# Graph layer and gated feed-forward: order of the left parts around the norm in the first phase

## The chip, the cores and the metric

One Trainium2 chip, one core. The metric is the device time of one execution in microseconds (us); the kernel before has 2005.67 us as the median of 3 runs (2003.96 to 2008.26).

## The reference

N = 10000 rows of D = 1024 numbers in float32, and 5000 edges (src, dst).

```
u   = layernorm(x)                            # per row
h   = u @ W.T + b                             # W 1024 x 1024
deg = 1 + count of src per row;  dis = deg ** -0.5
x1[i] = x[i] + sum over edges (i, j), with (i, i) added: dis[i] * dis[j] * h[j]
z   = layernorm(x1)
out = x1 + z @ base_W.T + base_b + z @ A_s.T @ B_s.T
      + sum over the best 2 of 6 experts: gate_e * (z @ A_e.T) @ B_e.T      # rank 16
```

## The kernel before

**Tiles and phases.** The rows are padded to 79 tiles of 128. The first phase makes, for every tile, the weighed rows h * dis (stored as `h_rows`, for the gathers) and the residual part (`r_rows`). The second phase gathers neighbours, normalises again and applies the feed-forward; it is not touched.

**Precision.** Every float32 matrix is split into a high part (a copy rounded to fp32r by ScalarE, `left_high`, `quarter_high`) and a low part (the difference, by VectorE, `left_low`, `quarter_low`). A product of high and low parts is three matmuls for each 128 rows of depth.

**The first phase.** The first HEAD = 7 tiles are done plainly: per tile, both halves of the output and all of depth, 48 matmuls (`single`). From tile 7 on, two tiles form a pair (36 pairs, `first(p) = 7 + 2p`), and a scheme of Strassen's kind needs 7 products of 512 x 512 blocks for 8. The left operands of a pair are A11, S1, S2, A12, S3, A22, S4, the right ones B11, T1, T2, B21, T3, T4, B22. The right sums T1 to T4 are made once, during the last plain tiles, by GpSimd (`quarter`), in four pieces of 128 x 512 each, then split by ScalarE and VectorE. A product is 12 matmuls (`product`, lines 1412 to 1416).

**The left operands.** For each tile: VectorE takes `statistics(t)`, GpSimd the power -1/2 of the variance (`rstd(t)`), VectorE makes `scales(t)`, ScalarE normalises the tile into `un` (`normalise(t)`, line 1048), and TensorE transposes it into the two banks `bt[0]` and `bt[1]` (line 1423), with `transpose_first(p)` for the first tile of a pair and `transpose_second(p)` for the other. From the first tile come A11 and A12. From the second, A21 is copied out of bt[0] (`second_row`), and A22 stays in bt[1] until both its parts are taken. `sums(p)` on VectorE makes S1, S2, S3, S4 and the low parts of S1 and S2; `sums_high(p)` on ScalarE the high parts of S1, S2 and A12; `others_high(p)` those of A22 and S3; `last_high(p)` that of S4. All are instructions at line 1089 (high) and 1892 (low).

**The order of TensorE** is fixed. Within pair p: S1, S2, first transposes of pair p+1, A12, S3, A11 of pair p+1, second transposes of pair p+1, A22, S4. The first transposes of p+1 wait for `un`, for A21 and for the low part of A22 of pair p, since they overwrite bt. S2 waits for a bank that ScalarE fills (`begin_second`).

**Queues.** Every engine runs its own list in order, with waits on semaphores. ScalarE's list for pair p, from the sums on: `begin_first(p+2)`, `begin_second(p+1)`, `second_row(p+1)`, `sums_high(p+1)`, `normalise(first(p+2))`, `weigh_part(p, C21, A22)`, `others_high(p+1)`, then `last_high(p+1)`. VectorE's, after `sums(p+1)`: statistics of first(p+2), low part of A12, scales of first(p+2), low parts of A22 and S3, then `finish_part`, S4, and the residual.

**Factors.** dis = deg ** -0.5 for 79 tiles is a power on GpSimd (`factors`, line 763), done in column groups FACTORS: tiles 0 to 7 at t = 2, the three others at t = 3, 4 and 5 of the plain tiles. VectorE makes sqd = deg * dis from it (line 1769). Pairs 1 to 20 also carry the ranking of edges (`ranks`) on VectorE, pairs 2 to 21 the counts on GpSimd, pair 22 the slot table, pair 24 the spill flag, which the transposes of the next pair wait for.

Of the kernel before, what the change touches and what calls it, by code (L numbers as in the profile page):

```python
# [10 lines left out]
ALU = mybir.AluOpType  # L11
# [7 lines left out]
TILES = -(-N // P)  # L19
# [34 lines left out]
HEAD = 7  # L54
# [26 lines left out]

T_AT = {T3: 4, T1: 8, T2: 12, T4: 16}

FACTORS = ((0, 8), (8, 32), (32, 56), (56, TILES))
RANK_AT, COUNT_AT, SLOT_AT, SCATTER_AT, TABLE_AT = 1, 2, 22, 23, 28


# [71 lines left out]
def gnn_ffn(nc, x, src, dst, w_t, b, base_t, b_low, router_b, out, deg_dram, spill_dram):  # L159
# [5 lines left out]
    with ExitStack() as ctx:  # L165
# [287 lines left out]
        def first(p):  # L453

            return HEAD + 2 * p
# [254 lines left out]
        def _(pool):  # L710
# [55 lines left out]
            for t in range(HEAD):  # L766
                if t == 2:
                    pool.wait_ge(deg_ok, 1)
                    factors(*FACTORS[0])
                rstd(t + 2)  # L770
                if t == 3:
                    pool.wait_ge(t_in[1], 16)
                    pool.wait_ge(t_in[0], 32)
                    quarter(wr_raw[T3], wr_raw[T3], wr_raw[T1], 0)
                if t == 4:
                    quarter(wr_raw[T1], wr_raw[T1], wr_high_raw[T1], 1)
                if 3 <= t < 3 + len(FACTORS) - 1:
                    factors(*FACTORS[t - 2])
                if t == 5:
                    pool.wait_ge(t_ok, 8)  # L780
                    pool.wait_ge(t_in[2], 32)
                    quarter(wr_raw[T2], wr_high_raw[T2], wr_raw[T1], 2)
                if t == 6:
                    pool.wait_ge(t_ok, 12)
                    quarter(t4, t4, wr_raw[T2], 3)
# [47 lines left out]
            for p in range(PAIRS):  # L833
                if p + 1 < PAIRS:
                    rstd(first(p + 1) + 1)
                if 0 <= p - COUNT_AT < CHUNKS // RANKED:
                    gather_counts(p - COUNT_AT)
                if SCATTER_AT <= p < SCATTER_AT + CHUNKS // 10:
                    c = 10 * (p - SCATTER_AT)
                    if p == SCATTER_AT:  # L840
                        pool.wait_ge(zero_stored, 64)
                        pool.wait_ge(slots_ok, 1)
                        carry_wait(12)
                    put_slots(range(c, c + 5))
                if p + 2 < PAIRS:
                    rstd(first(p + 2))
                if 0 <= p - COUNT_AT < CHUNKS // RANKED:
                    put_counts(p - COUNT_AT)
                if SCATTER_AT <= p < SCATTER_AT + CHUNKS // 10:
                    put_slots(range(c + 5, c + 10))  # L850
                if 0 <= p - PIECE_AT < PIECES:
                    differences(p - PIECE_AT)
# [186 lines left out]
        def _(act):  # L1039
# [134 lines left out]
            def weigh_sum(p, n, t, to, v, ok):  # L1174

                act.wait_ge(done, product_at(p, n))
                if p > 0:
                    act.wait_ge(part_ok[v], p)
                else:
                    act.wait_ge(t_lo_ok, 16)  # L1180
                nc.scalar.activation(to[:], bp[p % 2][1][:], ACT.Copy,
                                     scale=dis[:, first(p) + t:first(p) + t + 1]).then_inc(ok, 1)

            def weigh_part(p, v, n):

                t, h = PARTS[v]
                act.wait_ge(done, product_at(p, n))
                if p == 0:
                    act.wait_ge(dis_ok, len(FACTORS))
                    act.wait_ge(r_ok, HEAD - 1 + (t == 0))  # L1190
                    act.wait_ge(h_stored[t], 16 * ((HEAD - 1 - t) // 2 + 1))
                else:
                    act.wait_ge(part_stored[v], 16 * p)
                    act.wait_ge(pair_r_ok, 2 * (p - 1) + t + 1)
                nc.scalar.activation(hrow[t][:, half(h)], bp[p % 2][BANK[n]][:], ACT.Copy,
                                     scale=dis[:, first(p) + t:first(p) + t + 1]) \
                    .then_inc(part_ok[v], 1)
# [44 lines left out]
                    quarter_high(T2, wr_raw[T2])  # L1242
            second_row(0)
            sums_high(0)
            normalise(first(1))
            weigh(HEAD - 1)
            begin_second(0)
            others_high(0)
            begin_first(1)
            act.wait_ge(first_done, 2 * HEAD)  # L1250
            act.wait_ge(t_ok, 16)
            quarter_high(T4, t4)

            for p in range(PAIRS):
                last_high(p)
                if p == PAIRS - 1:
                    right_high(B11)
                weigh_sum(p, S2, 0, u2, C12, u2_ok)
                if p + 1 < PAIRS:
                    first_row(p + 1)  # L1260
                weigh_part(p, C11, A12)
                if p + 1 < PAIRS:
                    first_row_right(p + 1)
                    normalise(first(p + 1) + 1)
                    if p > 0:
                        begin_third(p + 1)
                weigh_sum(p, S3, 1, u3, C22, u3_ok)
                if p + 2 < PAIRS:
                    begin_first(p + 2)
                if p + 1 < PAIRS:  # L1270
                    begin_second(p + 1)
                    second_row(p + 1)
                    sums_high(p + 1)
                if p + 2 < PAIRS:
                    normalise(first(p + 2))
                weigh_part(p, C21, A22)
                if p + 1 < PAIRS:
                    others_high(p + 1)

            act.wait_ge(weights_in[7], 48)  # L1280
            nc.scalar.activation(narrow_hi[:], narrow_raw[:], ACT.Copy).then_inc(rest_hi_ok, 1)
# [423 lines left out]
        def _(dve):  # L1705
# [43 lines left out]
            def quarter_low(n, raw, at):  # L1749
                for k in range(4):  # L1750
                    dve.wait_ge(t_hi_ok, at + k + 1)
                    if n in (T1, T2):
# [2 lines left out]
                                            wr_hi[n][:, k, :].bitcast(F32), ALU.subtract) \  # L1755
                        .then_inc(t_lo_ok, 1)

            def finish_rows(t):

                if t == 0:  # L1760
                    dve.wait_ge(rows_in, 32)
                    dve.wait_ge(dis_ok, 1)
                    link(nc.vector.tensor_tensor(sqd[:, 0:HEAD], deg[:, 0:HEAD], dis[:, 0:HEAD],
                                                 ALU.mult))
                    nc.vector.tensor_tensor(b_step[:], b_rows[:, half(1)], b_rows[:, half(0)],
                                            ALU.subtract).then_inc(step_ok, 1)
                if t == HEAD - 1:
                    dve.wait_ge(dis_ok, len(FACTORS))
                    link(nc.vector.tensor_tensor(sqd[:, HEAD:TILES], deg[:, HEAD:TILES],
                                                 dis[:, HEAD:TILES], ALU.mult))  # L1770
                dve.wait_ge(h0_ok, 2 * (t + 1))
                nc.vector.scalar_tensor_tensor(hrow[t % 2][:], b_rows[:], dis[:, t:t + 1],
                                               hrow[t % 2][:], ALU.mult, ALU.add).then_inc(h_ok, 1)
                dve.wait_ge(h_ok, t + 1)
                nc.vector.scalar_tensor_tensor(xn[t % 6][:], xn[t % 6][:], sqd[:, t:t + 1],
                                               hrow[t % 2][:], ALU.mult, ALU.add).then_inc(r_ok, 1)
# [164 lines left out]
            for t in range(HEAD):  # L1941
# [21 lines left out]
                    columns()  # L1963
                if t == 4:
                    quarter_low(T3, wr_raw[T3], 0)
                if t == 5:
                    quarter_low(T1, wr_raw[T1], 4)
                if t == HEAD - 1:
                    left_low(0, A11, a11[:])
                    quarter_low(T2, wr_raw[T2], 8)  # L1970
            sums(0)
            statistics(first(1))
            left_low(0, A12, left_raw[A12][:])
            scales(first(1))
            left_low(0, A22, bt[1][:])
            dve.wait_ge(s3_ok, 1)
            left_low(0, S3, left_raw[S3][:])

            for p in range(PAIRS):
                if p == 0:  # L1980
                    finish_rows(HEAD - 1)
                    quarter_low(T4, t4, 12)
                else:
                    finish_part(p - 1, C12, S4, u2, u2_ok)
                left_low(p, S4, s4[:])
# [9 lines left out]
                    scales(first(p + 1) + 1)  # L1995
                if p > 0:
                    residual(p - 1, 1, (C22, C21))
                if RANK_AT <= p < RANK_AT + CHUNKS // RANKED:
                    ranks(p - RANK_AT)
                if p == SLOT_AT:  # L2000
# [4 lines left out]
                if p + 1 < PAIRS:  # L2005
                    sums(p + 1)
                    if p + 2 < PAIRS:
                        statistics(first(p + 2))
                    left_low(p + 1, A12, left_raw[A12][:])
                    if p + 2 < PAIRS:  # L2010
                        scales(first(p + 2))
                    left_low(p + 1, A22, bt[1][:])
                    dve.wait_ge(s3_ok, p + 2)
                    left_low(p + 1, S3, left_raw[S3][:])
            finish_part(PAIRS - 1, C12, S4, u2, u2_ok)
# [323 lines left out]
```

## Time and profile before

| | before |
|---|---|
| median of 3 runs | 2005.67 us |
| profiled execution, its own time | 2003.67 us |
| its span | 2001.5 us |
| TensorE busy | 1926.3 us, 96% |
| VectorE, ScalarE, GpSimd busy | 73%, 45%, 48% |
| granted TensorE clock, mean | 0.987 |
| plain tiles | to about 109 us |
| pairs | to about 880 us |
| second phase | the rest |

The granted clock is the share of full speed that TensorE got. A busy time counts an instruction from its start to its modelled end; matmuls overlap, so 390 ns of one is not its price: in sequence they start 0.23 us apart at full clock.

### The profile page before, as it was taken

How to read it: one execution, taken by the hardware profiler on the slowest of the kernel's cores; microseconds unless marked ns; L12 is line 12 of the kernel's file. 1: busy time of each engine (PE TensorE's matmuls, PEld its weight loads, DVE VectorE, ACT ScalarE, POOL GpSimd, SP SyncE). 2: the span in 40 equal slices, each digit the busy share in tenths (PEclk: the TensorE clock that was granted, in tenths of full speed). 3: DMA queues.
4: the chain of work that ended last, by engine and by line, in shares of the span. 5: the costliest groups of instructions: out<-in, count | busy, mean ns of one | idle time of the engine just before them, and what ended most of it. 6: DMA issues, size and time to landing. Idle time of an engine off the chain costs nothing.

```text
span 2001.5 us, 28823 instructions
## 1 busy us (share of the span) xinstructions
PE 1926.3 (96%) x9583; PEld 1613.6 (81%) x9583; DVE 1463.7 (73%) x3528; ACT 906.8 (45%) x1533; POOL 952.5 (48%) x963
## 2 busy tenths in 40 slices
PE   7989999999999999966999999999999999999999
PEld 6778777877787888855788888888888888888887
DVE  6878788878877667758677777767767766776775
ACT  4455555555555556543433433434343343434332
POOL 1712444354333520027655665656566665556640
PEclk9989999999999999987999999999999999999999
DMA  6624555545534444475333433333333333343321
GB/s 241 212 92 170 164 174 179 182 160 172 192 139 145 166 136 163 147 256 145 88 99 101 106 88 97 93 106 101 104 98 92 95 93 105 97 108 95 91 63 54
DMA packets 148969, 260.54 MB, mean 130 GB/s; under 512 B 56077, under 2 KB 75357, under 8 KB 148822
## 3 DMA queue, kind: packets, MB, share of 16 engines
q1 hardware_dynamic: 99478, 237.85, 34.1%
q0 software_dynamic: 49344, 20.85, 8.3%
q8 instruction: 77, 1.26, 0.3%
q14 instruction: 70, 0.57, 0.1%
HBM read 273.80 MB, written 129.74 MB: 202 GB/s over the span
## 4 chain that ended last, share of the span: by engine, by line
PE 63%; issue 19%; POOL 11%; DVE 4%; DMA 2%; ACT 1%; POOLq 0%; SPq 0%; DVEq 0%; ACTq 0%
PE bo L1552 13%; PE bo L1556 13%; PE bo L1554 13%; PE bt L1602 3%; POOL piece L829 3%; POOL counted L796 2%; PE bo L1412 2%; PE bo L1416 2%; PE bo L1414 2%; POOL xpw L738 2%; POOL counts L810 2%; PE bo L1570 2%; PE bo L1566 2%; PE bo L1568 2%; PE bo L1592 2%
## 5 line engine op out<-in xcount | busy, mean ns | idle before, releaser
L860 POOL DMA_INDIRECT acc<-h_rows,row_now x308 | 503.8, 1636 | 104.4 <-issue 101.7
L1412 PE MATMUL bo<-wr_hi,left_hi 128*128 128x512 f32 x1008 | 399.6, 396 | 4.8 <-ACT bo L1164 3.1
L1416 PE MATMUL bo<-wr_hi,left_lo 128*128 128x512 f32 x1008 | 393.7, 391 | 0.0
L1414 PE MATMUL bo<-wr_lo,left_hi 128*128 128x512 f32 x1008 | 393.0, 390 | 0.0
L738 POOL TENSOR_TENSOR xpw<-xpin,neg_half 128x1 f32<-128x1 f32 x79 | 72.7, 920 | 489.4 <-DVE xpin L1720 489.4
L1552 PE MATMUL bo<-wr_hi,sum_hi 128*128 128x512 f32 x624 | 248.2, 398 | 2.3 <-DVE sum_lo L2164 2.3
L1554 PE MATMUL bo<-wr_lo,sum_hi 128*128 128x512 f32 x624 | 244.6, 392 | 0.0
L1556 PE MATMUL bo<-wr_hi,sum_lo 128*128 128x512 f32 x624 | 244.4, 392 | 0.0
L1412 PEld LDWEIGHTS bo<-wr_hi,left_hi 128*128 128x128 f32 x1008 | 189.7, 188 | 42.9 <-issue 5.9
L1416 PEld LDWEIGHTS bo<-wr_hi,left_lo 128*128 128x128 f32 x1008 | 189.6, 188 | 40.2
L1414 PEld LDWEIGHTS bo<-wr_lo,left_hi 128*128 128x128 f32 x1008 | 189.8, 188 | 37.2
L948 POOL TENSOR_TENSOR pw<-pin,neg_half 128x1 f32<-128x1 f32 x79 | 73.6, 932 | 273.9 <-DVE pin L2081 262.2
L1048 ACT ACTIVATE un<-xn,xshift,xscale 128x1024 f32<-128x1024 f32 x79 | 98.3, 1244 | 229.3 <-issue 228.5
L1294 ACT ACTIVATE z_half<-acc,shift,scale 128x512 f32<-128x512 f32 x158 | 119.8, 807 | 91.5 <-DVE shift L2099 91.5
L1556 PEld LDWEIGHTS bo<-wr_hi,sum_lo 128*128 128x128 f32 x624 | 117.8, 189 | 25.6
L1552 PEld LDWEIGHTS bo<-wr_hi,sum_hi 128*128 128x128 f32 x624 | 117.7, 189 | 25.5 <-ACT row_hi L1301 3.0
L1554 PEld LDWEIGHTS bo<-wr_lo,sum_hi 128*128 128x128 f32 x624 | 117.9, 189 | 22.0
L1552 PE MATMUL bo<-wr_hi,right_hi 128*128 128x512 f32 x320 | 132.1, 413 | 0.2 <-DVE acc L2182 0.2
L1556 PE MATMUL bo<-wr_hi,right_lo 128*128 128x512 f32 x320 | 125.1, 391 | 0.0
L1554 PE MATMUL bo<-wr_lo,right_hi 128*128 128x512 f32 x320 | 124.7, 390 | 0.0
L2188 DVE TENSOR_TENSOR sum_raw<-bt,row_raw 128x512 f32<-128x512 f32 x39 | 27.0, 691 | 133.0 <-ACT row_raw L1337 133.0
L2173 DVE SCALAR_TENSOR_TENSOR acc<-acc,dis,bo 128x512 f32<-128x512 f32 x158 | 117.1, 741 | 4.3 <-PE bo L1596 3.1
(235 smaller groups left out, 4281.9 us busy)
## 6 DMA issues: line engine op xcount, KB each, us to landing
xn<-x SPq DMA_DIRECT2D x79, 512.0 KB, 3.9
r_rows<-xn SPq DMA_DIRECT2D x79, 512.0 KB, 3.3
acc<-r_rows SPq DMA_DIRECT2D x79, 512.0 KB, 4.4
out<-acc SPq DMA_DIRECT2D x79, 512.0 KB, 2.8
h_rows<-hrow SPq DMA_DIRECT2D x144, 256.0 KB, 2.3
acc<-h_rows,row_now POOLq DMA_INDIRECT x308, 4.3
wr_raw<-w_t SPq DMA_DIRECT2D x16, 256.0 KB, 6.4
piece<-base_t SPq DMA_DIRECT2D x64, 64.0 KB, 2.8
```

The lines of the kernel that those rows point to most:

```text
L738: nc.gpsimd.tensor_tensor(xpw[t % 2][:], xpin[t % 2][:], neg_half[:, 0:1], ALU.pow) \
L860: nc.gpsimd.indirect_dma_start(to[:], None, h_dram, bass.IndirectOffsetOnAxis(ap=at, axis=0), bounds_check=NPAD - 1, oob_is_err=False, com ...
L948: nc.gpsimd.tensor_tensor(pw[:], pin[:], neg_half[:, 0:1], ALU.pow) \
L1048: nc.scalar.activation(un[:], xn[t % 6][:], ACT.Identity, bias=xshift[t % 2][:], scale=xscale[t % 2][:]) \
L1294: ins = nc.scalar.activation(z_half[v][:], acc[a][:, half(v)], ACT.Identity, bias=shift[:], scale=scale[:])
L1412: nc.tensor.matmul(ps, left_hi[n][:, k, :], wr_hi[n][:, k, :], start=False, stop=False, skip_group_check=True)
L1414: nc.tensor.matmul(ps, left_hi[n][:, k, :], wr_lo[n][:, k, :], start=False, stop=False, skip_group_check=True)
L1416: last = nc.tensor.matmul(ps, left_lo[n][:, k, :], wr_hi[n][:, k, :], start=False, stop=(k == 3), skip_group_check=True)
L1552: nc.tensor.matmul(ps, y_hi[n][:, k, :], wr_hi[w][:, k, :], start=(begins and k == 0), stop=False, skip_group_check=True)
L1554: nc.tensor.matmul(ps, y_hi[n][:, k, :], wr_lo[w][:, k, :], start=False, stop=False, skip_group_check=True)
L1556: last = nc.tensor.matmul(ps, y_lo[n][:, k, :], wr_hi[w][:, k, :], start=False, stop=(k == 3), skip_group_check=True)
L2173: nc.vector.scalar_tensor_tensor(av, av, dis[:, bass.ds(t, 1)], bank, ALU.mult, ALU.add).then_inc(f_ok, 1)
```

## The change

- ScalarE, loop: `others_high(p+1)` stands directly behind `sums_high(p+1)`, ahead of `normalise(first(p+2))` and `weigh_part(p, C21, A22)`.
- VectorE, loop: the low part of A22 stands ahead of `scales(first(p+2))`.
- ScalarE, start: `begin_second(0)`, `others_high(0)` and T4's high parts stand ahead of the norm of tile 9 (`first(1)`), of `weigh(6)` and `begin_first(1)`.
- VectorE, start: T1's low parts move from t = 5 to t = 6; A12, A22 come ahead of the statistics of tile 9, S3 ahead of its scales; T4's low parts ahead of the rows of tile 6.
- GpSimd: the groups are tiles 0 to 7, 8 to 15, 16 to 47 and 48 to 78. The second is done at t = 3, the third and fourth in pairs 0 and 1, between the powers for two norms.
- sqd follows in two pieces; ScalarE waits on the factors' semaphore where it first needs each group.

```diff
-FACTORS = ((0, 8), (8, 32), (32, 56), (56, TILES))
+FACTORS = ((0, 8), (8, 16), (16, 48), (48, TILES))
+
+LATER_AT, LATER = (0, 1), (16 - HEAD) // 2
...
-                if 3 <= t < 3 + len(FACTORS) - 1:
-                    factors(*FACTORS[t - 2])
+                if t == 3:
+                    factors(*FACTORS[1])
...
+                if p in LATER_AT:
+                    factors(*FACTORS[2 + LATER_AT.index(p)])
                 if p + 2 < PAIRS:
                     rstd(first(p + 2))
...
                 else:
                     act.wait_ge(t_lo_ok, 16)
+                    act.wait_ge(dis_ok, 2)
+                if p == LATER:
+                    act.wait_ge(dis_ok, len(FACTORS))
...
                 if p == 0:
-                    act.wait_ge(dis_ok, len(FACTORS))
                     act.wait_ge(r_ok, HEAD - 1 + (t == 0))
...
             second_row(0)
             sums_high(0)
-            normalise(first(1))
-            weigh(HEAD - 1)
             begin_second(0)
             others_high(0)
-            begin_first(1)
             act.wait_ge(first_done, 2 * HEAD)
             act.wait_ge(t_ok, 16)
             quarter_high(T4, t4)
+            normalise(first(1))
+            weigh(HEAD - 1)
+            begin_first(1)
...
                     sums_high(p + 1)
+                    others_high(p + 1)
                 if p + 2 < PAIRS:
                     normalise(first(p + 2))
                 weigh_part(p, C21, A22)
-                if p + 1 < PAIRS:
-                    others_high(p + 1)
...
+            def later_factors(a, z, n):
+                dve.wait_ge(dis_ok, n)
+                link(nc.vector.tensor_tensor(sqd[:, a:z], deg[:, a:z], dis[:, a:z], ALU.mult))
...
                 if t == HEAD - 1:
-                    dve.wait_ge(dis_ok, len(FACTORS))
-                    link(nc.vector.tensor_tensor(sqd[:, HEAD:TILES], deg[:, HEAD:TILES],
-                                                 dis[:, HEAD:TILES], ALU.mult))
+                    later_factors(HEAD, FACTORS[2][0], 2)
...
-                if t == 5:
+                if t == HEAD - 1:
                     quarter_low(T1, wr_raw[T1], 4)
-                if t == HEAD - 1:
                     left_low(0, A11, a11[:])
                     quarter_low(T2, wr_raw[T2], 8)
             sums(0)
+            left_low(0, A12, left_raw[A12][:])
+            left_low(0, A22, bt[1][:])
             statistics(first(1))
-            left_low(0, A12, left_raw[A12][:])
-            scales(first(1))
-            left_low(0, A22, bt[1][:])
             dve.wait_ge(s3_ok, 1)
             left_low(0, S3, left_raw[S3][:])
+            scales(first(1))
+            quarter_low(T4, t4, 12)
...
                     finish_rows(HEAD - 1)
-                    quarter_low(T4, t4, 12)
...
+                if p == LATER - 1:
+                    later_factors(FACTORS[2][0], TILES, len(FACTORS))
...
                     left_low(p + 1, A12, left_raw[A12][:])
+                    left_low(p + 1, A22, bt[1][:])
                     if p + 2 < PAIRS:
                         scales(first(p + 2))
-                    left_low(p + 1, A22, bt[1][:])
```

## Rows read from the trace of the kernel before

**Rows 1.** Page, part 1: busy us, share of the span, instructions.

```profile
PE 1926.3 (96%) x9583; PEld 1613.6 (81%) x9583; DVE 1463.7 (73%) x3528; ACT 906.8 (45%) x1533; POOL 952.5 (48%) x963
```

**Rows 2.** Table by stretch: length, busy of each engine, PEclk, DMA share, GB/s.

```profile
101.40:108.20 6.80, 5.90 (x18) 5.03 (x19) 4.97 (x7) 4.11 (x8) 4.17 (x3) 0.50 0.32 107
...
118.50:121.90 3.40, 3.40 (x10) 2.51 (x9) 3.33 (x6) 2.95 (x6) 0.00 (x0) 0.50 0.14 58
...
142.70:599.60 456.90, 441.67 (x2101) 364.38 (x2101) 369.86 (x890) 251.68 (x400) 184.91 (x246) 1.00 0.50 170
```

**Rows 3.** Timeline of TensorE, start of the pairs: start, duration, instruction, idle before.

```profile
102.30 1.97 PE L1423 MATMUL bt<-ident,un 128*128 128x128 f32 x8 [3.19 <-ACT un L1048]
...
108.78 0.39 PE L1412 MATMUL bo<-wr_hi,left_hi 128*128 128x512 f32 x1
...
117.45 0.47 PE L1412 MATMUL bo<-wr_hi,left_hi 128*128 128x512 f32 x1 [3.07 <-ACT bo L1164]
```

**Rows 4.** Waits of TensorE, 142.7 to 853.3 us: total, times, longest.

```profile
PE bt L1423 <- DVE left_lo L1892: 16.2, 22, 1.1
PE bt L1423 <- DVE spill_flag L1989: 1.8, 1, 1.8
```

**Rows 5.** Timeline of TensorE: transposes, pairs 1, 2, 23, 34 and 35.

```profile
121.83 1.07 PE L1423 MATMUL bt<-ident,un 128*128 128x128 f32 x8
...
130.94 1.03 PE L1423 MATMUL bt<-ident,un 128*128 128x128 f32 x8
...
142.71 1.03 PE L1423 MATMUL bt<-ident,un 128*128 128x128 f32 x8
...
599.60 1.03 PE L1423 MATMUL bt<-ident,un 128*128 128x128 f32 x8
...
832.41 1.04 PE L1423 MATMUL bt<-ident,un 128*128 128x128 f32 x8
...
853.27 1.03 PE L1423 MATMUL bt<-ident,un 128*128 128x128 f32 x8
```

**Rows 6.** Timeline of ScalarE in a pair without stall.

```profile
589.93 1.88 ACT L1089 ACTIVATE left_hi<-left_raw 128x512 fp32r<-128x512 f32 x3 [0.82 <-DVE left_raw L1907]
596.37 1.25 ACT L1048 ACTIVATE un<-xn,xshift,xscale 128x1024 f32<-128x1024 f32 x1 [4.56 <-issue]
...
598.09 0.58 ACT L1089 ACTIVATE left_hi<-bt 128x512 fp32r<-128x512 f32 x1
```

**Rows 7.** Timeline of VectorE: A22's low part, pairs 5 and 6.

```profile
228.04 0.69 DVE L1892 TENSOR_TENSOR left_lo<-bt,left_hi 128x512 fp32r<-128x512 f32 x1 [2.42 <-ACT left_hi L1089]
...
250.15 0.69 DVE L1892 TENSOR_TENSOR left_lo<-bt,left_hi 128x512 fp32r<-128x512 f32 x1 [2.42 <-ACT left_hi L1089]
```

**Rows 8.** Timeline of GpSimd: powers for factors, and one for a norm.

```profile
46.51 1.65 POOL L763 TENSOR_TENSOR dis<-deg,neg_half 128x8 f32<-128x8 f32 x1 [18.36 <-DVE deg L1950]
...
77.88 4.62 POOL L763 TENSOR_TENSOR dis<-deg,neg_half 128x24 f32<-128x24 f32 x1
...
83.64 4.82 POOL L763 TENSOR_TENSOR dis<-deg,neg_half 128x23 f32<-128x23 f32 x1
...
138.06 0.93 POOL L738 TENSOR_TENSOR xpw<-xpin,neg_half 128x1 f32<-128x1 f32 x1 [10.34 <-DVE xpin L1720]
```

**Rows 9.** Timeline of VectorE in the last plain tiles and pair 0.

```profile
60.66 2.00 DVE L1772 SCALAR_TENSOR_TENSOR hrow<-b_rows,dis,hrow 128x1024 f32<-128x1024 f32 x1 [0.98 <-ACT hrow L1070]
...
86.25 0.16 DVE L1729 SCALAR_TENSOR_TENSOR xshift<-xmv,xscale 128x1 f32<-128x1 f32 x1
89.82 5.69 DVE L1754 TENSOR_TENSOR wr_lo<-wr_raw,wr_hi 128x512 fp32r<-128x512 f32 x4 [3.41 <-ACT wr_hi L1082]
...
107.25 0.68 DVE L1907 TENSOR_TENSOR left_raw<-bt,a 128x512 f32<-128x512 f32 x1
```

**Rows 10.** Timeline of ScalarE around tile 9's norm.

```profile
97.14 0.58 ACT L1109 ACTIVATE left_raw<-bt 128x512 f32<-128x512 f32 x1
...
114.43 1.24 ACT L1048 ACTIVATE un<-xn,xshift,xscale 128x1024 f32<-128x1024 f32 x1 [4.59 <-issue]
```

## The prediction

> **What bounds the kernel now.** I read the page's busy shares first: TensorE is busy 96% of the span [rows 1], so time can only come from its idle stretches and from stretches at a low clock. The table by stretch says where these lie inside the first phase. From 142.7 to 599.6 us the engine is busy 441.67 of 456.90 us at clock 1.00, so 15.2 us are idle; two short stretches near the start, 6.80 and 3.40 us, run at granted clock 0.50 [rows 2]. That is the lower of the engine's two levels, 1.2 GHz against 2.4, and each stretch comes with a stall, of 3.19 and of 3.07 us [rows 3]. The table of waits names what is late in the pair loop: 22 times the transposes wait for the low part of a left matrix, 16.2 us in all, and once for the spill flag, 1.8 us [rows 4]. All three are at the lines that the change moves.
>
> Below, "first transposes of pair p+1" are those that fill both banks bt again; they must wait until VectorE has read the A22 block of pair p out of bt[1], which it does in the low part of A22. "Second transposes" are the other tile's.
>
> **The loop's price now.** The first transposes of pairs 34 and 35 start at 832.41 and 853.27 [rows 5], 20.86 us apart with no wait, which I take as the period of an unhindered pair. From pair 2 (142.71) to pair 35 (853.27) there are 33 periods in 710.56 us; at 20.86 they would be 688.4. So 22.2 us are lost. (The waits of [rows 4] add up to 18.0; the rest is the array filling again, some 0.2 us after each.)
>
> **Why the low part is late.** A pair without the ranking work shows the queue on ScalarE: three high parts end at 591.81, it idles 4.56 us, does the norm at 596.37, weighs a part, and only at 598.09 takes A22's high part [rows 6]. The norm waited for its scales, which VectorE and GpSimd make from the statistics. VectorE in turn idles 2.42 us before A22's low part, in pairs with ranking too (228.04 and 250.15) [rows 7]. A22's high part needs nothing of the norm: its source is in bt[1] since the second transposes, and its buffer is free after one product that follows them. So it waits only because of its place in the queue.
>
> **Part 1, pair loop (others_high ahead of normalise; A22's low part ahead of scales).** In the pair of [rows 6], A22's high part would run at about 591.8 instead of 598.09, and its low part right behind A12's, near 595.4 instead of 598.7, where it follows the high part: 3.3 us earlier. The largest single wait is 1.1 us [rows 4], so all 22 go, with 2 us to spare. What is late next? First VectorE itself. In a ranking pair its cycle is 250.15 - 228.04 = 22.11 us, of which 2.42 is that idle time and about 0.5 the wait for the scales that A22's low part now fills: 19.2 us of work and short waits, under 20.86, so TensorE sets the period. Second the norm. It moves behind two more copies on ScalarE, 0.58 us and about 0.6, but these run in the 4.56 us in which ScalarE idled, so they cost nothing; if that cover were gone they would cost 1.2. The scales move behind one low part of 0.6 us, 0.5 of it inside the wait for GpSimd's power; net 0.15 to 0.6. The norm of [rows 6] ends at 597.6 and the transposes that need it start at 599.60 [rows 5]: 2.0 us of cover against 0.15 to 1.8. Third the spill flag (pair 24): VectorE's queue ahead of it gets about 1.1 us shorter, no more, since S4's high part still follows the norm; about 0.7 us of loss stays. A period's part between first and second transposes is 9.11 us early on (121.83 to 130.94) and some 0.04 less in the last pairs; over 22 pairs that is 0.9, which stays. Gain of the loop: 22.2 - 0.7 - 0.9 = 20.6 us. Bounds: 0 if VectorE's work and not its wait is what binds, 22.2 above; below nothing only by the norm, see the rivals.
>
> **Part 2, the start.** Four edits meet here, so I follow the queues.
> - GpSimd loses 16 columns of power at t=3, and all of those at t=4 and t=5. Eight columns take 1.65 us, 24 take 4.62 [rows 8], 0.19 a column, so about 3.0 + 4.6 + 4.8 us of its queue go. The quarter sums T2 and T4 start some 5 and 8 us sooner.
> - VectorE has the four low parts of T1 (5.69 us, at 89.82 [rows 9]) no longer ahead of the statistics of tile 8. What takes their place is the two row operations of tile 5, now near 93.7, which run 2.0 to 2.2 us each where GpSimd subtracts quarters beside them, as the one at 60.66 [rows 9]. Scales then near 98.0; ScalarE has its copy of A12 done at 97.7 (97.14 + 0.58) [rows 10]; norm to 99.3. TensorE reaches these second transposes at 102.30 - 3.19 = 99.1 and starts them at 99.4, 2.9 us sooner, without the drop to half clock. A11 of pair 0, now at 108.78 [rows 3], follows 0.8 us of transposes and 12 matmuls of 0.23 later: 103.0.
> - VectorE makes up T1's low parts (2.5), A11's (0.7) and T2's (2.5) from 98.0 to 103.7, so the sums start at 103.7, not 107.25 [rows 9], and S1 is ready 3.25 us on, behind four sums of 0.6 each and its low part of 0.7: 106.95. TensorE, through with A11 at 105.7, waits 1.2 for it: a new, smaller stall. S1 ends 109.7.
> - S2 waited 3.07 us for the second bank [rows 3], because ScalarE sat 4.59 us before the norm of tile 9 at 114.43 [rows 10]. begin_second now comes first; this stall and its half-clock stretch go. S2 ends at 112.4.
> - Then the norm of tile 9 is late. From 106.3 VectorE has five low parts (S1, S2, A12, A22, S3) and the statistics (1.9) ahead of its scales, to 111.3; GpSimd's power 111.7, scales 112.05, norm 113.35. First transposes of pair 1 at 113.45, against 121.83 [rows 5]: 8.4 us sooner, with a stall of 1.0.
> - VectorE goes on without a pause: low parts of T4 2.5, square roots 0.3, rows of tile 6 2.6, S4 0.6, statistics 1.9, A11 of pair 1 0.7: 120.7. TensorE wants it at 119.8, a last stall of 0.95. Second transposes of pair 1 at 123.5, against 130.94 [rows 5]: gain 7.4 us.
> - The powers of 32 and 31 columns, 5.5 to 6.1 us by the rates above, run on GpSimd in pairs 0 and 1 between two powers for norms; its idle time there is 10.34 us before 138.06 [rows 8]. Hidden; without cover they would cost up to 6 us each. Square roots of later tiles, done in pair 3: 0.2 us of VectorE, hidden by its idle time. The added waits on dis_ok are met long before, and nothing queues behind them. No DMA is added, and SyncE's order is as it was; row stores of tile 6 come no later than its queue needs.
>
> Bounds of this part: 2.9 (only S2's stall goes and tile 8's norm stays late) to 10.
>
> **Sum.** 7.4 + 20.6 = 28.0 us. The second phase starts from the last stores of the first and is shifted whole. The profiled execution took 2003.67 us, so 1975.7; the median of the runs is 2.0 above it, so the median forecast is 2005.67 - 28.0 = 1977.7.
>
> **A rule that speaks against it.** Beside the power of 23 columns (83.64 to 88.46), the scalar-tensor operation at 86.25, which reads two tiles of SBUF, took 0.16 us [rows 9]: not held at all; beside GpSimd's subtractions VectorE's low parts took 5.69 for four. The Trainium skill ("SBUF — State Buffer", "SBUF: two separate sides") says the port pair shared by VectorE and GpSimd is an exclusive lock for a whole instruction. By that the long powers would hold VectorE in pairs 0 and 1. The slowed low parts fit the rule; the power does not.
>
> **Rivals.**
> 1. The wait moves to the norm or to VectorE's work and half of the loop's gain stays: 1977.7 + 10.3 = 1988.0. For it: 65 norms wait for scales, and the ranking pairs leave VectorE only 1.7 us. Against: 2.42 us of idle time directly ahead of the late operation. 0.12.
> 2. At the start tile 8's norm stays late, since GpSimd's quarters now run beside VectorE's row operations: gain 2.9 instead of 7.4, 1982.2. 0.11.
> 3. The powers hold VectorE for 6 us in pairs 0 and 1, 2 of it covered each time: 8 us, 1985.7. The rule of the page named above would give this; the row at 86.25 speaks against. 0.03.
> 4. Slower: the norm slips in every pair. If it ends over 2.0 us later than now, each further us costs 34, once a pair. It needs ScalarE's 1.2 and VectorE's 0.6 in series and another 0.2 or more; at 3.0 us late the loop loses 34 in place of its present 22.2, and the start's 7.4 stay: 2005.7 - 7.4 - 22.2 + 34 = 2010. Against: 4.56 us of idle time. 0.05.
> 5. No effect: VectorE's order is not what binds, and the start only trades stalls. 2005.7. 0.03.
> The forecast itself has 0.66, with its own range 1973 to 1982.
>
> **Chances.** Faster by over 0.2% (4 us; less can't be told from no change here): 0.66 + 0.12 + 0.11 + 0.03 = 0.92. Within: 0.03. Slower: 0.05. The range reaches from 1973 (both upper bounds nearly) past rivals 2 and 3 to most of 1: 1989.
>
> **What would show it.** Right: no wait of the transposes for a low part between 120 and 850 us; a period of 20.86 to 20.9 in ranking pairs; the second transposes of pair 1 near 123.5; no stretch at clock 0.50 before 850 us; A22's high part directly behind A12's, with ScalarE's idle time before the norm shorter by 1.2. Wrong: waits for "un" at the first transposes of many pairs (rivals 1, 4), a stall of over 1 us near 99 (rival 2), or VectorE operations of several us beside the powers (rival 3).

## The result, and the profile after

| | before | changed |
|---|---|---|
| median | 2004.82 us (4 runs) | 1974.19 us (4 runs, 1973.28 to 1975.08) |
| ratio, 95% interval | | 0.984 (0.9829 to 0.9852) |
| span of the profiled run | 2001.5 us | 1972.0 us |

The forecast was 1977.7 us, within 1973 to 1989, faster. The time lies in the range, 1.2 us above its low end: 30.6 us were gained by the medians where 28.0 were forecast. Between the two profiled runs the span fell by 29.5 us.

The table by stretch, cut at the same events in both kernels: the first transposes of pair 0, the second of pair 1, the second of pair 35, and the end. Columns: stretch, length, busy time of TensorE, its weight loads, VectorE, ScalarE and GpSimd, granted clock, DMA share, GB/s. Before:

```profile
95.30:130.90 35.60, 29.34 (x121) 23.68 (x120) 26.74 (x48) 20.03 (x33) 10.08 (x7) 0.86 0.28 100
130.90:862.30 731.40, 713.45 (x3402) 590.45 (x3401) 564.13 (x1283) 407.64 (x645) 253.99 (x317) 1.00 0.48 160
862.30:2001.50 1139.20, 1100.93 (x5653) 931.66 (x5651) 801.60 (x2074) 439.38 (x793) 644.77 (x596) 0.98 0.38 103
```

After:

```profile
95.40:122.20 26.80, 25.35 (x122) 20.23 (x121) 23.35 (x45) 19.81 (x33) 5.10 (x4) 1.00 0.34 118
122.20:832.70 710.50, 709.55 (x3402) 592.37 (x3401) 562.67 (x1285) 405.39 (x646) 256.28 (x319) 1.00 0.50 166
832.70:1972.00 1139.30, 1099.99 (x5653) 931.52 (x5651) 801.27 (x2073) 439.50 (x793) 645.01 (x596) 0.98 0.37 103
```

The start is 8.8 us shorter, the loop 20.9, and what follows is as long as it was: the second phase is shifted whole. TensorE idles 0.95 us in 710.5 us of loop, and the start has clock 1.00 throughout, so both half-clock stretches of [rows 2] are gone. From pair 2 to pair 23 the first transposes now start 20.86 us apart, in every pair, ranking or not; that is the period of an unhindered pair in the prediction. I call the first length "the start" and the second "the loop" from here on.

The waits of TensorE after, from 90 to 850 us (total, times, longest), answer [rows 4]:

```profile
PE bt L1428 <- DVE spill_flag L1995: 1.0, 1, 1.0
PE bo L1417 <- issue: 0.9, 2, 0.6
PE bt L1428 <- ACT un L1052: 0.5, 1, 0.5
```

No transpose waits for a low part. The 0.9 and 0.5 us lie in the start. ScalarE in a ranking pair after (start, duration, instruction, idle before); it answers [rows 6]:

```profile
228.55 1.88 ACT L1093 ACTIVATE left_hi<-left_raw 128x512 fp32r<-128x512 f32 x3 [0.82 <-DVE left_raw L1914]
230.34 0.58 ACT L1093 ACTIVATE left_hi<-bt 128x512 fp32r<-128x512 f32 x1
230.81 0.62 ACT L1093 ACTIVATE left_hi<-left_raw 128x512 fp32r<-128x512 f32 x1
235.05 1.25 ACT L1052 ACTIVATE un<-xn,xshift,xscale 128x1024 f32<-128x1024 f32 x1 [3.62 <-issue]
```

A22's high part (from bt) runs directly behind the three others. The idle time before the norm has shrunk from 4.56 to 3.62 us (0.94, where 1.2 was the forecast sign): two copies went into time that was free. VectorE beside it, answering [rows 7]:

```profile
234.00 0.68 DVE L1899 TENSOR_TENSOR left_lo<-bt,left_hi 128x512 fp32r<-128x512 f32 x1
234.60 0.14 DVE L1733 COPY xscale<-xpw 128x1 f32<-128x1 f32 x1
```

Both the 2.42 us of idle time ahead of the low part [rows 7] and the 0.47 us ahead of the scales are gone. The latter stood in the trace before as:

```profile
225.28 0.15 DVE L1728 COPY xscale<-xpw 128x1 f32<-128x1 f32 x1 [0.47 <-POOL xpw L738]
```

At the start, TensorE after, answering [rows 3] and [rows 5]: second transposes of pair 0, A11, S1, first and second transposes of pair 1.

```profile
99.07 1.04 PE L1428 MATMUL bt<-ident,un 128*128 128x128 f32 x8
...
102.69 0.39 PE L1417 MATMUL bo<-wr_hi,left_hi 128*128 128x512 f32 x1
...
106.19 0.47 PE L1417 MATMUL bo<-wr_hi,left_hi 128*128 128x512 f32 x1 [0.61 <-issue]
...
112.44 1.09 PE L1428 MATMUL bt<-ident,un 128*128 128x128 f32 x8 [0.53 <-ACT un L1052]
...
122.18 1.04 PE L1428 MATMUL bt<-ident,un 128*128 128x128 f32 x8
```

The prediction had 99.4, 103.0, 106.95, 113.45 and 123.5 for these five.

### The profile page after: what moved, and what is told of

Its sections match the earlier page's. It is cut to its first block, busy times and chain, and to the rows that moved or that the text cites. A ratio compares the mean times of both kernels' runs of the same rounds, so it can differ in the third digit from the quotient of the medians.

```text
span 1972.0 us, 28823 instructions
## 1 busy us (share of the span) xinstructions
PE 1917.8 (97%) x9583; PEld 1612.4 (82%) x9583; DVE 1458.1 (74%) x3529; ACT 904.6 (46%) x1533; POOL 945.1 (48%) x963
## 3 DMA queue, kind: packets, MB, share of 16 engines
q8 instruction: 77, 1.26, 0.3%
## 4 chain that ended last, share of the span: by engine, by line
PE 91%; issue 2%; POOL 2%; DVE 1%; ACT 1%; DMA 0%; POOLq 0%; DVEq 0%; ACTq 0%
PE bo L1557 13%; PE bo L1561 13%; PE bo L1559 13%; PE bo L1417 11%; PE bo L1421 11%; PE bo L1419 11%; PE bt L1607 4%; PE bt L1428 3%; PE bo L1575 2%; PE bo L1571 2%; PE bo L1573 2%; PE bo L1597 2%; PE bo L1599 2%; PE bo L1601 2%; POOL wr_raw L760 1%
## 5 line engine op out<-in xcount | busy, mean ns | idle before, releaser
L1559 PEld LDWEIGHTS bo<-wr_lo,sum_hi 128*128 128x128 f32 x624 | 117.6, 189 | 21.9
```

Source lines behind the costliest of these rows:

```text
L1559: nc.tensor.matmul(ps, y_hi[n][:, k, :], wr_lo[w][:, k, :], start=False, stop=False, skip_group_check=True)
```

## The experiments

Beside each time stand the lengths of the start and the loop, read in its trace as above (before 35.6 and 731.4, changed 26.8 and 710.5). They tell apart what the times blur, but each comes from one profiled execution. Ratios are to the kernel before on the same chip, with their 95% interval.

**The two parts apart.** loop_only is the kernel before with this edit alone:

```diff
                     sums_high(p + 1)
+                    others_high(p + 1)
...
-                if p + 1 < PAIRS:
-                    others_high(p + 1)
...
+                    left_low(p + 1, A22, bt[1][:])
                     if p + 2 < PAIRS:
                         scales(first(p + 2))
-                    left_low(p + 1, A22, bt[1][:])
```

> The kernel before with the two moves inside the pair loop alone (A22's and S3's high parts ahead of the norm on ScalarE, A22's low part ahead of the scales on VectorE). Theory: the gain of the loop and that of the start simply add, because a late low part of A22 costs TensorE once per pair whatever the start was. The second transposes of pair 1 stay at 130.9 us, both stretches at half clock stay, no wait of the transposes for a low part is left; gain 20.9 us, 1983.9 against 2004.8. Rival: the ranking pairs only run without stall because the start left VectorE further ahead; then part of the waits stays and the gain is under 15 us, over 1990.

Measured: 1982.38 us, 0.9887 (0.9871 to 0.9904); start 36.9, loop 709.9. The loop gives up 21.5 us whatever the start was.

start_only is the changed kernel with that edit undone:

> The changed kernel with the two moves inside the pair loop undone; start and factors as changed. Theory: second transposes of pair 1 at 122.2 us, no stretch at half clock before 850 us, but the 22 waits for a low part (16 us) and the spill flag's 1.8 us are back; gain 8.8 us, 1996.0. Rival: the earlier start gives VectorE and ScalarE a lead that takes some waits away, gain over 12 us.

Measured: 1996.62 us, 0.9958 (0.9942 to 0.9975); start 26.8, loop 731.5. The waits before the transposes are back: 22 of them, 18.2 us in all, where there were 23 with 18.0 us before (the spill flag's included). The trace names the low part for 9 of them and nothing for the other 13. The two gains, 22.1 and 7.9 us by the medians, add to 30.0 of the 30.6: they are independent. The rival (a lead carries over) falls.

In loop_only the start is 1.3 us longer than before. The same two stalls (3.18 and 3.77 us there) came with half-clock stretches of 3.4 and 6.8 us instead of 6.8 and 3.4. All of the 1.3 us lies behind the second stall, where the longer stretch falls: from S2 to the second transposes of pair 1 it is 14.8 us (118.66 to 133.42), and 13.5 before (117.45 to 130.94):

```profile
104.50:107.90 3.40, 3.40 (x11) 2.68 (x10) 3.39 (x4) 2.02 (x4) 2.28 (x2) 0.53 0.51 154
107.90:118.20 10.30, 6.77 (x29) 4.93 (x27) 6.99 (x16) 4.35 (x7) 0.93 (x1) 0.99 0.01 2
118.20:125.00 6.80, 6.34 (x18) 5.11 (x19) 5.87 (x9) 4.45 (x9) 0.00 (x0) 0.52 0.35 140
```

**Which engine's order pays in the loop.** late_scales takes back VectorE's half of the edit:

```diff
                     left_low(p + 1, A12, left_raw[A12][:])
-                    left_low(p + 1, A22, bt[1][:])
                     if p + 2 < PAIRS:
                         scales(first(p + 2))
+                    left_low(p + 1, A22, bt[1][:])
```

> The changed kernel with VectorE's order in the loop as before: A22's low part behind the scales of the next norm; ScalarE's order stays changed. Theory: ScalarE's order is the whole of the loop's gain. A22's low part comes 0.7 to 0.9 us later in each pair but still over 2 us ahead of the transposes; VectorE idles 0.45 us more for GpSimd's power, its cycle in ranking pairs near 19.7 us, under TensorE's 20.86. Time as changed, 1974.2 within 1. Rival: VectorE's order carries a part of it; then waits of up to 0.5 us come back in the ranking pairs, 1979 to 1984.

Measured: 1973.52 us, 0.9843 (0.9826 to 0.9859); start 26.8, loop 709.7, no wait of TensorE in the loop. With ScalarE's order changed, VectorE's half of the edit adds nothing that can be measured. (VectorE's half alone can't run: its low part of A22 would wait for ScalarE's high part, which stands behind the norm, which waits for the scales, which would stand behind that low part.)

**How much cover the norm has.** The fourth rival said that it slips. norm_late5 and norm_late10 put 5 and 10 useless copies of S3's high part ahead of the real one, and so ahead of the norm, in 34 pairs:

```diff
                 free_after(p, S3)
+                if p > 1:
+                    act.wait_ge(s3_ok, p + 1)
+                    for i in range(5):
+                        nc.scalar.activation(left_hi[S3][:].rearrange("p k n -> p (k n)"),
+                                             left_raw[S3][:], ACT.Copy).then_inc(ends_ok, 1)
+                        act.wait_ge(ends_ok, 5 * (p - 2) + i + 2)
                 left_high(p, S3, left_raw[S3][:], s3_ok, p + 1)
```

(norm_late10 has 10 in place of both 5s.)

> The changed kernel with five further copies of S3's high part on ScalarE ahead of the real one, in 34 pairs; they delay the norm. Theory: the norm waits for its scales, not for ScalarE, and has 3.6 us of idle time before it; five copies with their waits take about 3.5 us. The norm moves by 0 to 0.3 us, which the 2 us before the transposes cover: 1974.2 within 1. Rival: ScalarE's queue ahead of the norm is on the path; then each pair costs up to 3.5 us, 2090.

> The changed kernel with ten further copies of S3's high part ahead of the real one in 34 pairs. Five took 3.5 us and cost nothing. Theory (a cover of 2 us behind ScalarE's 3.6 us of idle time): ten take 7 us, the norm ends 3.4 us later than in the changed kernel, 1.4 us after TensorE is ready for the first transposes; with the array's filling again 1.6 us a pair, 54 us in all: 2028, within 15. Rival: the cover is larger, since everything else would shift with it: under 10 us lost. Other rival: the second norm and S4 slip too and each pair costs the full 3.4 us, 2090.

Measured: 5 copies 1974.35 us, 0.9842 (0.9825 to 0.9858), loop 709.5; 10 copies 2029.92 us, 1.0117 (1.0101 to 1.0132), loop 762.8. ScalarE with 5 copies:

```profile
230.48 3.28 ACT L1146 ACTIVATE left_hi<-left_raw 128x512 fp32r<-128x512 f32 x5
233.79 0.63 ACT L1093 ACTIVATE left_hi<-left_raw 128x512 fp32r<-128x512 f32 x1
234.72 1.25 ACT L1052 ACTIVATE un<-xn,xshift,xscale 128x1024 f32<-128x1024 f32 x1 [0.29 <-DVE xshift L1740]
```

with 10 copies, and TensorE's waits with 10:

```profile
238.94 6.60 ACT L1146 ACTIVATE left_hi<-left_raw 128x512 fp32r<-128x512 f32 x10
245.57 0.63 ACT L1093 ACTIVATE left_hi<-left_raw 128x512 fp32r<-128x512 f32 x1
246.11 1.22 ACT L1052 ACTIVATE un<-xn,xshift,xscale 128x1024 f32<-128x1024 f32 x1
```

```profile
PE bt L1434 <- ACT un L1052: 40.0, 30, 1.9
PE bt L1434 <- DVE spill_flag L2001: 3.2, 1, 3.2
```

Five use up the idle time (0.29 us left of 3.62) and cost nothing. Ten make the time 55.6 us longer than five do, against 54 forecast for ten; 53.3 us of it lie in the loop, 1.6 a pair, and the rest behind the loop, where no experiment looked. In the changed kernel the norm ends 1.95 us before the transposes that need it, in nearly every pair; with ten copies it ends 0.05 us before them. So the cover is the idle time plus this 1.95 us, and the mechanism of rival 4 (the norm slips) is real, but lay far off.

**The powers beside VectorE.** power_beside adds, in pairs 4 to 19, a power of 28 columns whose result is not used:

```diff
+                if 4 <= p < 20:
+                    nc.gpsimd.tensor_tensor(tick_pool[:, 16:44], deg[:, 0:28],
+                                            neg_half[:, 0:28], ALU.pow)
                 if p + 2 < PAIRS:
                     rstd(first(p + 2))
```

> The changed kernel with a further power of 28 columns on GpSimd (result not used) in each of pairs 4 to 19, between the powers for two norms. Theory: a power on GpSimd does not hold VectorE; it takes about 4.8 us of GpSimd's idle time, VectorE's operations beside it keep their length, time as changed, 1974.2 within 1. Rival (exclusive lock of the shared port for a whole instruction): VectorE's operations with two operands in SBUF wait up to 4.8 us in each of 16 pairs, of which about 2 are covered: some 40 us more, 2015.

Measured: 1974.15 us, 0.9837 (0.9821 to 0.9854); start 26.8, loop 709.6. GpSimd's power, and VectorE's operations inside it:

```profile
203.85 5.13 POOL L850 TENSOR_TENSOR tick_pool<-deg,neg_half 128x28 f32<-128x28 f32 x1
```

```profile
205.69 0.75 DVE L1879 SCALAR_TENSOR_TENSOR hrow<-bo,dis,u 128x512 f32<-128x512 f32 x1
207.21 0.69 DVE L1917 TENSOR_TENSOR left_raw<-bt,a 128x512 f32<-128x512 f32 x1 [0.77 <-ACT a L1123]
207.94 0.69 DVE L1922 TENSOR_TENSOR left_raw<-left_raw,a 128x512 f32<-128x512 f32 x1
```

The last has both operands in SBUF and took 0.69 us, its length without a power beside it. The Trainium skill ("SBUF — State Buffer", "SBUF: two separate sides") states that a VectorE operation with two SBUF inputs and a GpSimd operation that reads SBUF exclude each other for the whole instruction. This power reads SBUF and the rule does not hold for it; rival 3 is out. VectorE's low parts do get slower beside GpSimd's 512-column subtractions, below.

**What the start's 8.8 us are made of.** Three kernels take parts of the start back. t1_early moves T1's low parts back to t = 5:

```diff
-                if t == HEAD - 1:
+                if t == 5:
                     quarter_low(T1, wr_raw[T1], 4)
+                if t == HEAD - 1:
                     left_low(0, A11, a11[:])
```

> The changed kernel with T1's low parts back at t = 5 on VectorE, ahead of the statistics of tile 8. Theory: since GpSimd's quarters are now early, T1's high parts are ready near 88.9 and the low parts no longer wait 3.4 us; they end near 93.5, scales of tile 8 near 98.5, second transposes of pair 0 near 100.0 instead of 99.07, sums near 103.3 instead of 102.75: 0.5 to 1 us lost, 1975. Rival: the place of T1's low parts is what freed tile 8's norm; then the second transposes come at 102 again, with a half-clock stretch, and over 4 us are lost.

Measured: 1974.04 us, 0.9841 (0.9824 to 0.9857); start 27.7, loop 709.6. That is 0.9 us in the trace, under what the time can tell. The second transposes of pair 0 start at 98.80, without a stall, though T1's low parts are again ahead of tile 8's statistics: T1's place is worth little once the factors have moved.

early_factors puts the powers back into the plain tiles and keeps all orders (its groups there are 8, 32 and 31 columns, where the kernel before had 24, 24 and 23):

```diff
-                if t == 3:
-                    factors(*FACTORS[1])
+                if 3 <= t < 3 + len(FACTORS) - 1:
+                    factors(*FACTORS[t - 2])
...
-                if p in LATER_AT:
-                    factors(*FACTORS[2 + LATER_AT.index(p)])
```

> The changed kernel with the power of the later factors back in the plain tiles on GpSimd (8, 32 and 31 columns at t = 3, 4 and 5). Theory: the quarter sums T2 and T4 move back by 5 to 6 us; T2's does no harm, but T4's then runs until about 102 beside T1's low parts, which take about 5 us instead of 2.5: sums at 105 instead of 102.75, about 2.3 us lost, 1976.5. Rival: the place of the factors does not matter and T1's place does: less than 0.5 us lost.

Measured: 1977.48 us, 0.9856 (0.984 to 0.9872); start 31.7, loop 709.5: 4.9 us lost in the trace, twice the forecast (by the ratios 3 us). The second transposes of pair 0 have a stall again:

```profile
101.36 1.09 PE L1426 MATMUL bt<-ident,un 128*128 128x128 f32 x8 [1.25 <-ACT un L1050]
```

GpSimd in this kernel:

```profile
78.84 5.89 POOL L765 TENSOR_TENSOR dis<-deg,neg_half 128x32 f32<-128x32 f32 x1
...
85.96 5.27 POOL L765 TENSOR_TENSOR dis<-deg,neg_half 128x31 f32<-128x31 f32 x1
91.21 6.99 POOL L760 TENSOR_TENSOR wr_raw<-wr_high_raw,wr_raw 128x512 f32<-128x512 f32 x4
98.16 0.54 POOL L740 TENSOR_TENSOR xpw<-xpin,neg_half 128x1 f32<-128x1 f32 x1
98.67 6.43 POOL L760 TENSOR_TENSOR t<-t,wr_raw 128x512 f32<-128x512 f32 x4
```

and VectorE:

```profile
93.03 1.80 DVE L1777 SCALAR_TENSOR_TENSOR hrow<-b_rows,dis,hrow 128x1024 f32<-128x1024 f32 x1 [3.86 <-ACT hrow L1072]
94.86 2.19 DVE L1780 SCALAR_TENSOR_TENSOR xn<-xn,sqd,hrow 128x1024 f32<-128x1024 f32 x1
98.74 0.15 DVE L1731 COPY xscale<-xpw 128x1 f32<-128x1 f32 x1 [1.68 <-POOL xpw L740]
98.93 1.05 DVE L1732 SCALAR_TENSOR_TENSOR xshift<-xmv,xscale 128x1 f32<-128x1 f32 x1
99.90 5.76 DVE L1757 TENSOR_TENSOR wr_lo<-wr_raw,wr_hi 128x512 fp32r<-128x512 f32 x4
```

The norm's power stands behind T2's subtractions (VectorE waits 1.68 us for it), then T1's low parts run beside T4's subtractions and take 5.76 us instead of 2.5. This accounts for the loss: up to the start of T1's low parts VectorE has lost 1.7 us against the changed kernel (99.90 against 97.32, in a trace that runs 0.9 us later as a whole), and the stretched low parts add 3.3. In the changed kernel the powers are out of the way and T4's subtractions are over at 96.1, before T1's low parts begin:

```profile
90.04 6.02 POOL L760 TENSOR_TENSOR t<-t,wr_raw 128x512 f32<-128x512 f32 x4
...
119.61 5.43 POOL L765 TENSOR_TENSOR dis<-deg,neg_half 128x32 f32<-128x32 f32 x1
```

factors_only is the reverse: factors moved and the loop changed, both queues' start orders as before:

> The changed kernel with both queues' start orders as before (ScalarE: norm of tile 9 and weigh(6) ahead of begin_second and A22; VectorE: T1's low parts at t = 5, A22 and T4 late); the factors stay moved and the loop stays changed. With early_factors (orders changed, factors back, 4.9 us lost at the start) it splits the start's 8.8 us. Theory: S2's stall of about 3 us and its half-clock stretch are back, the norm of tile 8 is still earlier than before; from the first transposes of pair 0 to the second of pair 1 about 31 us (35.6 before, 26.8 changed): 4 us lost, 1978. Rival: the factors' place is nearly the whole of the start's gain and the orders add little: under 1.5 us lost.

Measured: 1980.25 us, 0.9873 (0.9858 to 0.9888); start 32.7, loop 709.5: 5.9 us lost, where 4 were expected. S2's stall is back, and the granted clock is 0.50 for 6.8 us from 112.0, near its end. But the second transposes of pair 0 start without a stall, and T1's low parts, which stand ahead of tile 8's statistics as before, take 2.97 us instead of 5.69 [rows 9]. TensorE (second transposes of pair 0, S2) and VectorE (T1's low parts):

```profile
98.86 1.05 PE L1428 MATMUL bt<-ident,un 128*128 128x128 f32 x8
...
113.69 0.77 PE L1417 MATMUL bo<-wr_hi,left_hi 128*128 128x512 f32 x1 [3.78 <-ACT bo L1168]
```

```profile
88.76 2.97 DVE L1759 TENSOR_TENSOR wr_lo<-wr_raw,wr_hi 128x512 fp32r<-128x512 f32 x4 [1.88 <-ACT wr_hi L1086]
```

The stall of 3.19 us ahead of these transposes [rows 3] thus goes with the factors alone, while the orders alone (early_factors) leave 1.25 us of it. Of the start's 8.8 us the factors alone bring 2.9 (35.6 to 32.7), the orders alone 3.9 (35.6 to 31.7), and together 2.0 more than their sum.

**Further gains.** flag_early puts the spill flag's two instructions ahead of `finish_part`:

```diff
             for p in range(PAIRS):
+                if p == SLOT_AT + 2:
+                    dve.wait_ge(max_done, 1)
+                    link(nc.vector.tensor_reduce(over_max[0:1, :], bt[0][0:1, 0:P], AX.X, ALU.max))
+                    nc.vector.tensor_copy(spill_flag[:], over_max[0:1, :]).then_inc(tables_ok, 1)
                 if p == 0:
...
                 left_low(p, S4, s4[:])
-                if p == SLOT_AT + 2:
-                    dve.wait_ge(max_done, 1)
-                    link(nc.vector.tensor_reduce(over_max[0:1, :], bt[0][0:1, 0:P], AX.X, ALU.max))
-                    nc.vector.tensor_copy(spill_flag[:], over_max[0:1, :]).then_inc(tables_ok, 1)
```

> The changed kernel with VectorE's two instructions for the spill flag (pair 24) ahead of finish_part and of S4's low part. Theory: TensorE's one wait left in the loop (0.95 us before the transposes at 615.0) goes and nothing takes its place: about 1.1 us less, 1973.1. Rival: the reduction waits for its source and holds VectorE, so the stall moves: no gain or a loss of up to 1 us.

Measured: 1973.91 us, 0.9849 (0.9833 to 0.9866); start 26.7, loop 709.4. No wait is left, but most of the other profiles with the flag in its old place show none either (late_scales: loop 709.7), so the time gained nothing measurable. Pair 24 takes 21.02 us here, 21.11 to 21.42 in those profiles and 22.12 in the changed kernel's, where VectorE's sums of that pair started late, for no reason that the trace names.

fill_idle fills the idle time that VectorE still had before the rows of tile 5:

```diff
                 if t != 2:
                     statistics(t + 2)
+                if t == HEAD - 1:
+                    statistics(first(1))
...
+                    second_row(0)
                     act.wait_ge(t_ok, 12)
                     quarter_high(T2, wr_raw[T2])
-            second_row(0)
...
                     left_low(0, A11, a11[:])
-                    quarter_low(T2, wr_raw[T2], 8)
             sums(0)
+            quarter_low(T2, wr_raw[T2], 8)
             left_low(0, A12, left_raw[A12][:])
             left_low(0, A22, bt[1][:])
-            statistics(first(1))
+            scales(first(1))
             dve.wait_ge(s3_ok, 1)
             left_low(0, S3, left_raw[S3][:])
-            scales(first(1))
```

> A try to improve on the changed kernel at the start: VectorE takes the statistics of tile 9 in its 3.9 us of idle time before the rows of tile 5 (at 88.8), ScalarE copies A21 ahead of T2's high parts, VectorE makes the sums ahead of T2's low parts. Theory: the stalls of 0.61 (S1) and 0.53 us (first transposes of pair 1) go, and VectorE, which bounds the start, is 1.9 us further: second transposes of pair 1 1.5 us earlier, 1972.7; seen in the trace, hardly in the time. Rival: T2's low parts become the wait of S2 and what is gained at S1 is lost there: no change.

Measured: 1972.61 us, 0.983 (0.9817 to 0.9844); start 24.8, loop 710.6 (the flag's wait was there, 0.96 us). The start has no stall left. The edit of both is these two together:

> fill_idle and flag_early together. Theory: they add, since they touch different pairs: start as in fill_idle (24.8 us from the first transposes of pair 0 to the second of pair 1, 26.8 changed), and no wait for the spill flag in any run, where two of the profiles so far showed 0.95 us and the others none. Some 2 to 3 us less than changed: ratio to before 0.983, 1971.5 to 1972.5. Rival: nothing of the 2 us survives to the end, since the second phase waits for something not shifted: ratio 0.9845.

Measured: 1970.21 us (1969.37 to 1971.02), 0.9825 (0.9812 to 0.9838); start 24.8, loop 709.4. TensorE's only wait from 90 to 850 us stands at 848.4, behind the loop:

```profile
PE bo L1417 <- ACT u L1188: 0.9, 1, 0.9
```

Start and loop together are 3.1 us shorter than the changed kernel's in the traces (734.2 against 737.3); 1.1 of it is pair 24, long in that one profile. Both kernels beat the one before clearly. The two were not timed side by side: their times do not overlap (1969.37 to 1971.02 against 1973.28 to 1975.08), but the intervals of their ratios do, so that the combined version is faster than the changed kernel is likely, and shown by the traces better than by the times.

## Where the prediction held, and which step of it failed

- **What bounds the loop**: right. TensorE waited for A22's low part because of its place in ScalarE's queue. The loop lost 22.2 us by the working; it gave back 20.9 in the profiled run and 21.5 to 22.0 in nine other profiles with ScalarE's new order in the loop (709.4 to 709.9, two of them with the flag moved).
- **The step that failed** is in the start, in two parts. The first is the cause of tile 8's late norm. The prediction has it freed because T1's low parts no longer stand ahead of its statistics, and prices the factors' powers as queue time on GpSimd, with no term of their own in the 7.4 us. The runs showed that the factors alone do it, and T1's place alone does not. With T1's low parts in their old place (factors_only, t1_early) the second transposes of pair 0 start without a stall, at 98.86 and 98.80; with T1's low parts moved but the powers back (early_factors) a stall of 1.25 us stays. T1's place is worth 0.9 us, the factors' 4.9 of the 8.8, since with the powers in the plain tiles GpSimd's subtractions run beside VectorE's low parts and stretch them from 2.5 to 5.8 us.
- **The second part is the size of the start's term**: 7.4 forecast, 8.8 measured. The rows of tile 5 on VectorE were put at 93.7, with no working given; they ran at 92.7, when ScalarE had weighed them (91.43 + 1.24). VectorE stayed 1 us ahead of the working through the sums of pair 0 (102.75 against 103.7) and the scales of tile 9 (111.1 against 112.05), and the queue behind these took 0.35 us less than its sum. The stalls forecast at 1.2, 1.0 and 0.95 us came as 0.61, 0.53 and 0.31.
- **The 0.9 us "which stays"** did not; no reason was given for it. Before, the stalled ranking pairs had 9.10 to 9.12 us between first and second transposes; after, the same pairs have 9.05 or 9.06. Stalled again in norm_late10, they have 9.12 to 9.14. The difference was the stall's own tail, and this term should have been zero.
- **The flag's 0.7 us**: pair 24 was 1.26 us longer than the period in the profiled run and 0.25 to 0.6 in seven others. With the item above this is the loop's miss: 20.6 forecast, about 21.9 usual.
- **The norm's cover**: right (2.0 us by the working, 1.95 measured), tested from both sides.
- **The powers in the pairs**: hidden, as forecast; 5.43 us for 32 columns against 5.5 to 6.1.
- **Rivals**: none happened. The total came within 2.6 us because the loop, three quarters of it, was right in mechanism; that the start came out near as well owes something to luck, since both its edits were in the change and only their split was wrong. The time lies 1.2 us above the low end of a range that reaches 15 us further up.

## What to carry to other kernels

Where an in-order queue shows an instruction that waits for nothing but the one ahead of it, move it over that wait. The gain is the stall it causes downstream, once per round, and the cost is zero as long as the idle time it moves into is longer. Read the cover from two times, when the result is ready and when it is wanted, and add the idle time ahead (here 1.95 and 3.62 us): five copies stayed within it and ten did not. For work off the critical path, ask what runs beside it when it moves: the powers mattered because they pushed the subtractions onto VectorE's low parts.

## What the runs showed of the hardware

- A power on GpSimd did not slow VectorE: 28 columns took 5.13 us, and a VectorE operation with two operands in SBUF inside it took 0.69 us, as without. GpSimd's subtractions of 128x512 beside the low parts stretched four of these from 2.50 to 5.76 us, and an operation on one column from 0.16 to 1.05.
- Stalls of 3.19 and 3.07 us at the start (before), of 3.18 and 3.77 (loop_only) and of 3.78 us (factors_only) each came with granted clock 0.50, for 3.4 or 6.8 us, which set in between 1.7 us before the stall's end and 1.1 us after it; which length came differed between kernels with the same stall. Stalls of up to 1.9 us, in some 30 pairs of norm_late10, had one such stretch among them (3.4 us from about 587 us, clock 0.51). A stall of 2.66 us in early_factors and one of 3.23 us in norm_late10 had none.
- In two profiles (the changed kernel and fill_idle) VectorE's sums of pair 24 started some 1 us late with no releaser in the trace. What delayed them is open.
